# The output bias of four attention rows as a product on TensorE, with the norm reading PSUM

## What is computed

```
x = x + layernorm(attention(layernorm(x)))     # attention ends with  a @ wo.T + bo
x = x + layernorm(experts(layernorm(x)))       # 8 experts, top 1, and a shared one
```

```
y  = a @ wo.T + bo
x1 = x + (y - mean(y)) / sqrt(var(y) + 1e-5)
```

## Time and profile before

| what | value |
|---|---|
| median of 3 runs | 421.07 us (421.01 to 421.08) |
| the profiled execution | 420.75 us, of it span 418.9 us |
| TensorE busy | 397.9 us (95%) |
| VectorE busy | 274.7 us (66%) |
| ScalarE busy | 207.1 us (49%) |
| GpSimd busy | 122.9 us (29%) |
| chain that ended last | TensorE 81%, VectorE 9%, "issue" 3%, ScalarE 3%, GpSimd 2% |

### The profile page before, as it was taken

How to read it: one execution, slowest core, us unless ns; L and a number is a source line. 1 busy time by engine, 2 the same in 40 slices (tenths; PEclk the granted TensorE clock), 3 DMA queues, 4 the chain that set the end, 5 groups by cost and what they waited for, 6 DMA issues and landing times.

```text
span 418.9 us, 9551 instructions
## 1 busy us (share of the span) xinstructions
PE 397.9 (95%) x3443; PEld 301.6 (72%) x3443; DVE 274.7 (66%) x644; ACT 207.1 (49%) x381; POOL 122.9 (29%) x179
## 2 busy tenths in 40 slices
PE   8998999999999999898989999999999999999992
PEld 8775557676767766575768999999995444489991
DVE  5565677987879777877674694222225898736786
ACT  2745748586776757556551113444447766411110
POOL 2424514335152525303402002211222220015651
PEclk9999999999999999999999999999999999999998
DMA  8735235373634636360146750011111111114532
GB/s 259 220 109 151 64 84 189 92 228 89 217 90 123 193 87 211 101 196 1 55 140 204 246 189 27 27 50 52 52 50 39 52 40 39 40 47 120 152 113 75
DMA packets 50772, 47.29 MB, mean 113 GB/s; under 512 B 5350, under 2 KB 45542, under 8 KB 50726
## 3 DMA queue, kind: packets, MB, share of 16 engines
q1 hardware_dynamic: 44795, 38.31, 30.7%
q0 software_dynamic: 1632, 4.46, 3.7%
q10 hardware_dynamic: 4299, 3.92, 2.8%
HBM read 25.19 MB, written 8.65 MB: 81 GB/s over the span
## 4 chain that ended last, share of the span: by engine, by line
PE 81%; DVE 9%; issue 3%; ACT 3%; POOL 2%; DVEq 0%; ACTq 0%; POOLq 0%
PE bank L1420 41%; PE bank L1752 7%; PE bank L1424 6%; PE bank L1597 6%; PE bank L1617 5%; PE bank L1558 4%; PE bank L1777 3%; DVE nmax L1087 2%; PE bank L1496 2%; PE bank L1544 2%; PE bank L1433 2%; PE bank L1486 1%; DVE wall L1117 1%; DVE stats_at L991 1%; POOL rstd_at L644 1%
## 5 line engine op out<-in xcount | busy, mean ns | idle before, releaser
L1087 DVE TENSOR_REDUCE nmax<-bank 128x2 f32<-128x512 f32 x112 | 74.3, 686 | 27.3 <-PE bank L1558 26.7
L1420 PEld LDWEIGHTS bank<-stacks,wall 128*128 128x128 f32 x512 | 59.8, 192 | 2.5 <-issue 1.9
L1420 PE MATMUL bank<-stacks,wall 128*128 128x128 f32 x512 | 61.2, 276 | 0.4 <-ACT stacks L909 0.4
L1293 DVE TENSOR_TENSOR stacks<-stacks,bank 128x512 f32<-128x512 f32 x34 | 23.3, 687 | 53.3 <-PE bank L1420 50.8
L873 ACT ACTIVATE pv<-bank 128x512 f32<-128x512 f32 x64 | 38.2, 603 | 34.1 <-PE bank L1617 33.2
L909 ACT ACTIVATE stacks<-bank 128x512 f32<-128x512 f32 x34 | 20.3, 597 | 64.2 <-PE bank L1420 49.6
L873 ACT ACTIVATE wall<-bank 128x512 f32<-128x512 f32 x64 | 38.3, 606 | 24.9 <-PE bank L1617 24.8
L1617 PE MATMUL bank<-stacks 99*128 99x256 bf16 x256 | 48.8, 274 | 1.4 <-ACT wall L873 0.9
L1420 PE MATMUL bank<-wall,stacks 128*128 128x256 f32 (+1 forms) x208 | 49.2, 380 | 0.0
L1558 PE MATMUL bank<-stacks 96*128 96x256 bf16 x224 | 42.3, 273 | 4.8 <-DVE nmax L1087 4.7
L716 POOL DMA_INDIRECT stacks<-x_sc,row_i x18 | 20.3, 1125 | 89.2 <-PE bank L1424 70.1
(11 more groups left out here) (212 smaller groups left out, 795.0 us busy)
## 6 DMA issues: line engine op xcount, KB each, us to landing
stacks<-low_sb SPq DMA_DIRECT2D x144, 64.0 KB, 2.0
wall<-gate_up SPq DMA_DIRECT2D x8, 1024.0 KB, 5.5
wall<-down SPq DMA_DIRECT2D x8, 512.0 KB, 6.6
y_exp<-stacks ACTq DMA_DIRECT2D x18, 128.0 KB, 1.7
x_tok<-wall SPq DMA_DIRECT2D x8, 256.0 KB, 2.5
stacks<-x_tok SPq DMA_DIRECT2D x16, 128.0 KB
out<-stacks SPq DMA_DIRECT2D x8, 256.0 KB, 2.4
stacks<-low_sb SPq DMA_DIRECT2D x12, 128.0 KB, 2.4
```

The lines of the kernel that those rows point to most:

```text
L1087: dve.tensor_reduce(nmax[:, half, qt, 2 * pair:2 * pair + 2], two(sm_bank[u % 2]), AX.X, ALU.max, negate=True).then_inc(sm["sm_max"], 1)
L1293: dve.tensor_tensor(to, sg, fu[:, :], ALU.mult).then_inc(sm["h_sb"], 1)
L1420: last = pe.matmul(out_ap, lhsT, rhs, start=(n == 0), stop=(n == len(pairs) - 1))
```

## The change

In rows 4 to 7 (`b >= B - 4`) VectorE's sum with the bias is left out. TensorE adds the bias instead: behind the two products of each token tile comes a third into the same PSUM region, of a row of 128 ones (`ones_row`, one partition) with the row `bo_sb`. So each `D_wo` of these rows has six products. `ones_row` is written once by GpSimd at the start. Statistics and norm read bank `w2` in place of `y_sb`, so that `w2` stays in use until the norm is done; the norm still writes `y_sb`, and now waits there for the last row's `x1_ready`. What waited for `y_ready` waits for `yn_ready` in these rows (`wo_bank_read`). The turned maxima M0 of rows 6 and 7 go to bank `w0` in place of `w2`, and the products of ones that run into `w0` wait for ScalarE's copy of them (`mT_sb`).

```diff
         def m_bank(b, half):
-            return w0 if (b, half) == (B - 1, 1) else w2
+            return w0 if (b, half) in ((B - 2, 0), (B - 1, 0), (B - 1, 1)) else w2
+        def bias_in_products(b):
+            return b >= B - 4
+        def wo_bank_read(eng, rows):
+            eng.wait_ge(*((sm["yn_ready"], TB * rows) if bias_in_products(rows - 1) else (sm["y_ready"], rows)))
...
+            pool.memset(ones_row[:, :], 1.0).then_inc(sm["setup_pool"], 1)
...
+            def y_of(b, t):
+                return two(w2)[:, t, :] if bias_in_products(b) else y_sb[:, t, :]
+
             def d_wo(b, par):
                 dve.wait_ge(sm["wo_ps"], b + 1)
-                if counted(b):
-                    dve.wait_ge(sm["x1_ready"], b)
-                dve.tensor_tensor(y_sb[:, :, :], two(w2), bo_sb[:, :].unsqueeze(1).to_broadcast([P, TB, D]),
-                                  ALU.add).then_inc(sm["y_ready"], 1)
-                dve.wait_ge(sm["y_ready"], b + 1)
-                ln_head("at", b, lambda t: y_sb[:, t, :], stats["at"], lambda t: mv["at"][:, t, :], None, TB)
+                if not bias_in_products(b):
...
+                ln_head("at", b, lambda t: y_of(b, t), stats["at"], lambda t: mv["at"][:, t, :], None, TB)
...
             def d_yn(b, par):
                 dve.wait_ge(sm["at_rstd"], b + 1)
+                if bias_in_products(b):
+                    dve.wait_ge(sm["x1_ready"], b)
                 for t in range(TB):
-                    dve.scalar_tensor_tensor(y_sb[:, t, :], y_sb[:, t, :], mv["at"][:, t, 0:1],
+                    dve.scalar_tensor_tensor(y_sb[:, t, :], y_of(b, t), mv["at"][:, t, 0:1],
...
                     if counted(2 * b):
                         pe.wait_ge(sm["mT_sb"], 2 * b)
+                elif b >= B - 2:
+                    pe.wait_ge(sm["k_sb"], 2 * B)
+                    pe.wait_ge(sm["mT_sb"], 2 * b)
                 else:
-                    pe.wait_ge(sm["y_ready"], b - 1)
+                    wo_bank_read(pe, b - 1)
...
                     pe.wait_ge(sm["k_sb"], 2 * B)
+                    pe.wait_ge(sm["mT_sb"], 2 * b + 3)
                     ones_on(8, w0)
...
             def d_wo(b, par):
                 pe.wait_ge(sm["aT_sb"], b + 1)
+                bias = []
+                if bias_in_products(b):
+                    pe.wait_ge(sm["setup_pool"], 3)
+                    bias = [(ones_row[0:1, :], bo_sb[0:1, :])]
                 for t in range(TB):
                     last = products(two(w2)[:, t, :], [(aT[:, k, P * t:P * t + P], wo_sb[:, k, :])
-                                                       for k in range(KT)])
+                                                       for k in range(KT)] + bias)
```

More of the change, by code:

```diff
@@ L206, in program @@
         row_i = sb("row_i", [P, NR], I32)
+        ones_row = sb("ones_row", [P, P])
         pos_cur = sb("pos_cur", [P, 2], I32)
@@ L1101, in divide @@
                 return f
+            def y_of(b, t):
+                return two(w2)[:, t, :] if bias_in_products(b) else y_sb[:, t, :]
             def d_wo(b, par):
                 dve.wait_ge(sm["wo_ps"], b + 1)
-                if counted(b):
-                    dve.wait_ge(sm["x1_ready"], b)
-                dve.tensor_tensor(y_sb[:, :, :], two(w2), bo_sb[:, :].unsqueeze(1).to_broadcast([P, TB, D]),
-                                  ALU.add).then_inc(sm["y_ready"], 1)
-                dve.wait_ge(sm["y_ready"], b + 1)
-                ln_head("at", b, lambda t: y_sb[:, t, :], stats["at"], lambda t: mv["at"][:, t, :], None, TB)
+                if not bias_in_products(b):
+                    if counted(b):
+                        dve.wait_ge(sm["x1_ready"], b)
+                    dve.tensor_tensor(y_sb[:, :, :], two(w2), bo_sb[:, :].unsqueeze(1).to_broadcast([P, TB, D]),
+                                      ALU.add).then_inc(sm["y_ready"], 1)
+                    dve.wait_ge(sm["y_ready"], b + 1)
+                ln_head("at", b, lambda t: y_of(b, t), stats["at"], lambda t: mv["at"][:, t, :], None, TB)
                 dve.tensor_scalar(var["at"][:, :], mv["at"][:, :, 1], EPS, None, ALU.add
@@ L1637, in f @@
                         pe.wait_ge(sm["o_copied"], 2 * b + 2)
[L1638 to L1641, removed]
+                        if b >= B - 2:
+                            wo_bank_read(pe, b)
                         elif b >= 1:
@@ L1676, in d_xn2T @@
                 else:
-                    pe.wait_ge(sm["y_ready"], b + 1)
+                    wo_bank_read(pe, b + 1)
                 for k in range(KT):
```

## The result

| | median | from, to | profiled execution |
|---|---|---|---|
| before | 421.07 us | 420.45 to 421.32, 5 runs | 420.75 us |
| changed | 426.02 us | 425.82 to 427.59, 5 runs | 425.82 us |

A forecast was written before the change was run, and what follows sets the result against it. TensorE, busy 397.9 of 418.9 us, was taken to bound the kernel; rows 4 and 5 cost 1.60, row 6 1.52, row 7 1.62, together +4.74 on 421.07: 425.8 us (range 424.9 to 426.6; 8 in 10: 422.8 to 427.0).

The forecast's parts named there:

- The price of a product: TensorE's D_wo: two added products cost 1.52 us per row in rows 4 to 6, 1.62 in row 7; low end 0.87.
- one row behaves as the 32-row shape: TensorE's bias products: one row is run as 32, so shape changes are paid, 1.52 us per row instead of 0.87.
- PSUM reads at nothing: VectorE's statistics and norm reading PSUM: no change taken, at worst 0.01 us per row.
- Slot 5: Row 4's D_wo and the stretch behind: products cost 1.52 us, the dropped sum brings back 0.72, net 0.80.
- the 0.2 us of cover: Behind the ones: the SM step, done by 171.5, precedes maxima due at 171.7, so its delay costs nothing.
- Slot 6: Row 5's D_wo and the stretch behind: same pattern as row 4's, 1.52 us less 0.72, net 0.80.
- I set it at nothing: The ones' new wait for ScalarE's copied maxima in slots 5 and 6: 0.8 us long, taken as costing nothing.
- Rows 6 and 7: nothing comes back: Slot 7 and tail: dropped sum brings nothing, TensorE's path waits elsewhere; full 1.52 and 1.62 us are paid.
- The sum: Whole kernel: 1.60 for rows 4 and 5, 1.52 for row 6, 1.62 for row 7, together +4.74 us.
- Nothing comes back: Rival, slots 5 and 6: the new wait holds back the SM step, no relief; +6.18, 427.2 us; chance 0.11.
- No change of shape: Rival: one-row products pay by columns only, 0.87 us per row; +2.04, 423.1 us; chance 0.18.
- Faster: Rival: one-row products slip under their neighbours and cost nothing, relief stays; -1.44, 419.6 us; chance 0.04.

The follow-up runs named there:

- drop_only: The changed kernel with the bias left out altogether in rows 4 to 7, no bias products and no sum: 420.08 us, ratio 0.9971.
- full_rows: The changed kernel with the bias products over all 128 rows of the array (ones of 1/128, bias on every partition): 423.8 us, ratio 1.0064.
- rows45: The change made for rows 4 and 5 alone, rows 6 and 7 as in the kernel before: 423.23 us, ratio 1.0046.
- rows67: The change made for rows 6 and 7 alone, rows 4 and 5 as in the kernel before: 424.55 us, ratio 1.0073.
- product_only: The kernel before, VectorE's sum kept, with one-row products of zeros added to D_wo of rows 4 to 7: 427.37 us, ratio 1.015.
- no_ones: The changed kernel without the products of ones in slots 5 and 6 and their wait for the copied maxima: 426.73 us, ratio 1.0132.
- adjacent: The changed kernel with both one-row bias products of a row next to each other behind the four others: 425.3 us, ratio 1.0091.

## Why the prediction was right, point by point

- **What bounds.** Right. TensorE's extra work went into the time in full except in rows 4 and 5; VectorE's 2.3 us of saved work brought some 1.2 (drop_only's intervals).
- **The price of a product.** Right: 1.54 per row against 1.52, 1.65 at row 7 against 1.62 (5.02 - 3.37, and again in the experts' part). The view that decided was that of 64-row products among full ones. The step that one row behaves as the 32-row shape was a choice; it holds, with a form of its own, 1\*128, and the first record of each pair at 0.48 us. One row is also no faster than 32: its shorter records take 374 ns. Full shape gives 0.87 at row 7 (full_rows), the price by columns. A visit to the other shape costs 0.38 us in front of float32 and 0.29 in front of bfloat16, and nothing is left of it with full rows. The rule of the Trainium skill, "TensorEngine Tiling (Array Packing)", Key Properties, that a change of the tiling mode drains TensorE, agrees with these prices; that it is a drain which takes the time, no row here shows.
- **PSUM reads at nothing.** Right: 0.75 us for two statistics and 0.88 us for two norms either way.
- **Slot 5.** Right in the sum, 0.83 against 0.80, by a cover other than the one named. I had the step of 170.96 ready for its maxima at 171.7; it starts at 172.01 without a wait for them, so the 0.2 us of cover had failed. The working compared the wrong step with them: the one at 171.1 is the first SM step behind the ones (measured 171.12), and between it and the one that needs these maxima stand the scores of a head and eight more ones, 172.01 - 171.12 = 0.89 us. The later wait, 0.57 before and 0.27 now, took the 0.30 up; the prediction had counted it as room for TensorE's added time, not for this. So the zero of slot 5 holds in part by luck. The waits foretold as near 0, 0.3 and 0.6 were 0, 0 and 0.27.
- **Slot 6.** Here the same step was wrong: "I set it at nothing" was worth 0.25 us, on the path over ScalarE's copy that I hadn't followed. Only xn2T's wait was looked at as the next late thing. The text's own price for a failed cover, up to 0.72 per slot, held this. No run shows a loss as large.
- **Rows 6 and 7: nothing comes back.** Right: the wait for exponentials is 0.96 before and after, and dropping the sum alone changes 6 to 7 by 0.00. In the tail VectorE's shared products are late with TensorE's, as forecast. M0 in its new bank and the bank held until the norm cost nothing that rows45 and rows67 show (18.45 us from 6 to 7 in the one, 21.49 and 17.31 in the slots before in the other: the old distances). GpSimd's memset lies ahead of all intervals; it ran at 0.77 us, long before GpSimd's first power at 4.40.
- **The sum.** 0.83 + 1.08 + 1.55 + 1.70 = 5.16 us in the intervals; predicted were 0.80 + 0.80 + 1.52 + 1.62 = 4.74. The 0.25 and the last interval's 0.08, of which 0.05 arises in the experts' part, make up most of the rest. The median, +4.95, comes closer to 4.74 than the intervals do, and that is luck: the spread of executions is larger than the difference. The rivals are out by more than their times. "Nothing comes back" since the new wait holds back the SM step: drop_only has that wait and gets 0.73 and 0.46 us back. (product_only, where nothing comes back since the sum is still there, shows what such a kernel takes, 427.37 beside the 427.2 worked out.) "No change of shape" is what full_rows measures, 423.8 beside 423.1. "Faster", with the product hidden under its neighbours, fails at 1.54 us per row.

## What to carry to other kernels

A one-row product for a bias is not small on TensorE: it costs its columns, and between full products a change of shape on top (0.29 to 0.38 us here); spread the row over all 128 partitions and scale it, and split it into bfloat16 parts where float32's two records are too dear. Move work from VectorE to TensorE only in the stretches where TensorE waits for VectorE, and leave it elsewhere. When a new wait is set at nothing because a later one takes it up, follow each path that branches off in between, not only the one that was late before.

## What the runs showed that I had not expected

- The mean granted clock goes as low as 0.989 in some executions without the ones, though the traced ones show nothing of it.
- The start of the kernel moves single runs more than the change in slot 6 did. The piece of the chain that is the landing of a part of `x` (start, length) in the profiled executions of the changed kernel, of no_ones and of adjacent:

```profile
2.10 5.42 DMA x_sb<-x
```

```profile
2.11 6.87 DMA x_sb<-x
```

```profile
2.11 7.58 DMA x_sb<-x
```

The same transfer of the same code takes 2.2 us longer in one than in another, and row 4's D_wo starts at 163.37, 164.82 and 165.51, so the delay passes on in full. In the trace of before no transfer stands in the chain at the start. This is why the traced execution of no_ones takes longer than that of the changed kernel though its slots are shorter, and why the table above was needed; the other executions have no trace, so that their spread has the same source is not shown. What makes the transfer late is open.
